# Value parts of an exact linear-attention stage: GpSimd's work given to VectorE, ScalarE and TensorE, pair by pair of key tiles

## The reference

```python
q, k, v = heads(x @ Wq + bq), heads(x @ Wk + bk), heads(x @ Wv + bv)
q_proj, k_proj = proj(q), proj(k)      # gelu(x @ W1 + b1) @ W2 + b2, to 16 columns: one number per token and head
# both centred by their mean over tokens and divided by a common std
Z = concatenate([k_proj, q_proj])      # one key per token and head
vc = v - mean(v over tokens)
context(i) = sum over k_j < q_i of vc_j * (q_i - k_j)      # written as a sort and cumulative sums
norm(i)    = 2 * sum over k_j < q_i of (q_i - k_j) - (q_i * count - sum of k)
out = 2 * context / max(norm, 1e-4)
```

## Time and profile before

| | |
|---|---|
| median of three runs | 1470.56 us (1470.32 to 1474.03) |
| profiled execution, its own time | 1472.39 us |
| its span, first to last instruction | 1470.8 us |
| TensorE, VectorE, ScalarE, GpSimd busy | 74%, 65%, 55%, 45% |
| granted TensorE clock, mean | 0.882 of full |

### The profile page before, as it was taken

How to read it: one execution, slowest core, us unless ns; L and a number is a source line. 1 busy time by engine, 2 the same in 40 slices (tenths; PEclk the granted TensorE clock), 3 DMA queues, 4 the chain that set the end, 5 groups by cost and what they waited for, 6 DMA issues and landing times. The chain is left out here.

```text
span 1470.8 us, 30026 instructions
## 1 busy us (share of the span) xinstructions
PE 1088.7 (74%) x12088; PEld 893.4 (61%) x12088; DVE 957.1 (65%) x1553; ACT 811.8 (55%) x909; POOL 664.6 (45%) x648
## 2 busy tenths in 40 slices
PE   5364789368989899909998986465547965976698
PEld 2153665368888897609888883254227962642597
DVE  4212645799999975489999996223833644764365
ACT  6211443389999933249999995322523325653233
POOL 3744000736666640174666662745072440327244
PEclk9688799779999999959999997777778996987799
DMA  9777200402122100101212112265333433003343
GB/s 259 281 212 249 76 1 0 184 30 88 59 88 83 65 1 0 53 9 59 88 59 88 63 56 87 105 203 171 105 130 88 123 105 116 1 1 112 95 127 102
DMA packets 84587, 140.59 MB, mean 96 GB/s; under 512 B 10574, under 2 KB 71246, under 8 KB 79950
## 3 DMA queue, kind: packets, MB, share of 16 engines
q1 hardware_dynamic: 70276, 102.15, 21.8%
q0 software_dynamic: 13056, 35.87, 6.7%
q10 hardware_dynamic: 1120, 0.66, 0.2%
HBM read 86.62 MB, written 56.27 MB: 97 GB/s over the span
## 5 line engine op out<-in xcount | busy, mean ns | idle before, releaser
L1186 ACT ACTIVATE b_signs<-b_q_everywhere,normed 128x2048 bf16<-128x2048 f32 x224 | 429.8, 1991 | 23.6 <-PE banks L1096 20.7
L1096 PE MATMUL banks<-b_value_parts,b_signs 128*128 128x102 bf16 x8192 | 392.1, 209 | 38.7 <-DVE b_signs L1332 36.1
L1096 PEld LDWEIGHTS banks<-b_value_parts,b_signs 128*128 128x128 bf16 x8192 | 376.0, 97 | 61.8 <-DVE b_signs L1332 56.1
L1332 DVE TENSOR_SCALAR b_signs<-b_q_everywhere,normed 128x2048 bf16<-128x2048 f32 x288 | 395.9, 1435 | 1.6 <-PE banks L1096 1.6
L558 POOL DMA_INDIRECT moe_slots<-normed,slot_of_token x128 | 124.7, 974 | 39.3 <-issue 33.2
L1390 POOL TENSOR_TENSOR normed<-b_sums,normed 128x16 f32<-128x16 f32 x32 | 35.0, 1095 | 135.0 <-DVE b_sums L1343 135.0
L371 PE MATMUL banks<-identity,normed 128*128 128x128 f32 x256 | 51.5, 337 | 57.6 <-ACT normed L347 57.6
L1366 POOL TENSOR_TENSOR b_signs<-b_signs,normed 128x1024 f32<-128x1024 f32 x8 | 22.0, 2755 | 157.6 <-DVE normed L1282 157.1
L320 DVE BATCH_NORM_STATS2 ln_stats<-residual 128x6 f32<-128x256 f32 x192 | 71.1, 417 | 21.5 <-SPq L1589 10.5
L1088 PE MATMUL banks<-normed,ones_bf 128*128 128x408 bf16 x128 | 28.9, 350 | 69.5 <-DVE normed L1300 69.5
L380 PE MATMUL banks<-normed_T,wg 128*8 128x256 f32 x256 | 77.8, 433 | 0.0
(11 more groups left out here) (254 smaller groups left out, 2424.2 us busy)
## 6 DMA issues: line engine op xcount, KB each, us to landing
b_q_everywhere<-q_rows SPq DMA_DIRECT2D x32, 1024.0 KB, 4.7
normed<-expert_rows SPq DMA_DIRECT2D x6, 1024.0 KB, 10.4
d_rows<-moe_slots SPq DMA_DIRECT2D x40, 129.5 KB, 2.2
f_rows<-moe_slots SPq DMA_DIRECT2D x40, 129.5 KB, 2.2
moe_slots<-a_empty SPq DMA_DIRECT2D x8, 518.0 KB, 10.1
a_rows<-moe_slots SPq DMA_DIRECT2D x16, 259.0 KB, 3.6
moe_empty_slots<-a_empty SPq DMA_DIRECT2D x8, 518.0 KB, 5.5
moe_slots<-moe_empty_slots SPq DMA_DIRECT2D x1, 4144.0 KB
```

Of the source, the lines that this page charges most:

```text
L1096: ins = nc.tensor.matmul(banks[qt // QPB][:, qt % QPB * VP:(qt % QPB + 1) * VP], t.SG[:, (hh * TB + kt) % RING, qt * P:(qt + 1) * P], t.VO ...
L1186: nc.scalar.activation(t.SG[:, g % RING, :], t.QB[:, hh % 2, :], ACT.Sign, bias=t.NKT[:, kt, hh % H:hh % H + 1]).then_inc(s.sign_a, 1)
L1332: nc.vector.tensor_scalar(t.SG[:, g % RING, :], t.QB[:, hh % 2, :], t.KTM[:, kt, hh % H:hh % H + 1], 2.0, ALU.is_gt, ALU.mult).then_inc(s. ...
```

## The change

The row work of GpSimd in the preparation goes. The values of a pair of key tiles are held in a PSUM bank (seven banks in turn), with the centring row already added there by a bf16 product of a matrix with ones in its first three rows (`ROWS3B`) and the row's three parts in three partitions (`ROWP`, made by `dve_row`). Per pair, ScalarE copies the high part out of the bank; VectorE writes the product with k (`VZ`) and the rest of the values (`VR`, four slots); ScalarE writes both middle parts and the product's high part; TensorE makes rest minus middle part in the same bank by an f32 product with the identity and a bf16 one with its negative (`MINUSI`), and ScalarE copies that out as the third part; VectorE writes the product's third part. The column of k itself is split once for all tiles, and GpSimd only sets the columns of ones. The totals are 64 products with ones or minus ones over the finished parts (`pe_held`), ahead of head 0's first product, into banks 4 to 7; VectorE reduces and splits them behind its sign of tile 6 (`dve_held`). The products that add the totals stand ahead of tile 15 in each head and no longer ahead of tile 0. Scores of k are normed and transposed first, those of q later; SyncE's first broadcast waits for these. At the start GpSimd makes three constants more.

```diff
@@ program start, GpSimd
+    nc.gpsimd.memset(k.MINUSB[:, :], -1.0)
...
+    nc.gpsimd.tensor_copy(k.ROWS3B[:, :], k.LAYERF[:, 0, :])
+    nc.gpsimd.tensor_scalar(k.MINUSI[:, :], k.IDENT[:, :], -1.0, None, ALU.mult)
@@ pe_prepare, TensorE
-    pe_values(k, batch, 0)
-    pe_values(k, batch, 1)
+    pe_parts(k, batch)
+def pe_parts(k, batch):
+    nc.tensor.wait_ge(s.row, batch + 1)
+    for p in range(4):
+        pe_value(k, batch, p)
+    nc.tensor.wait_ge(s.zk, batch + 1)
+    for tile in range(TB):
+        ins = nc.tensor.transpose(k.bank[4][:, tile * H:(tile + 1) * H], t.Z[:, 1, tile * P:(tile + 1) * P], k.IDENT[0:H, 0:H])
+    ins.then_inc(s.zkt, 1)
+    pe_value(k, batch, 4)
+    for n in range(PAIRS + 1):
+        if n == 1:
...
+            for tile in range(TB):
...
+        if n + 5 < PAIRS:
+            if n + 5 >= 7:
+                nc.tensor.wait_ge(s.a_third, at + n - 1)
+            pe_value(k, batch, n + 5)
+        if n >= 1:
+            nc.tensor.wait_ge(s.a_mid, at + n)
+            nc.tensor.matmul(value_bank(k, n - 1)[:, :], k.IDENT[:, :], t.VR[:, (n - 1) % 4, :], start=True, stop=False)
+            nc.tensor.matmul(value_bank(k, n - 1)[:, :], k.MINUSI[:, :], value_columns(t, n - 1, False, 1), start=False,
+                             stop=True).then_inc(s.a_left, 1)
+def pe_held(k, batch):
...
+    for tiles, lo, hi, ones in ((ACT_KT, 0, 2 * DH, k.ONESB), (DVE_KT, 2 * DH, VC, k.MINUSB)):
+        for tile in tiles:
+            for b in range(4):
...
@@ pe_head
-        nc.tensor.wait_ge(s.held_parts, batch + 1)
...
+        pe_held(k, batch)
...
     for kt in range(TB):
+        if kt == TB - 1:
+            if h == 0:
+                nc.tensor.wait_ge(s.held_parts, batch + 1)
+            for bank in banks:
...
@@ act_prepare, ScalarE
+    for p in range(4):
+        act_part(k, batch, p, 0)
+    for n in range(PAIRS + 1):
...
+        if n < PAIRS:
+            act_product(k, batch, n, 0)
+            if n + 4 < PAIRS:
+                act_part(k, batch, n + 4, 0)
+            act_part(k, batch, n, 1)
+        if n >= 1:
+            act_product(k, batch, n - 1, 1)
+            act_part(k, batch, n - 1, 2)
@@ dve_prepare, VectorE
+    for n in range(PAIRS + 2):
+        if n < PAIRS:
+            nc.vector.wait_ge(s.a_hi, at + n + 1)
...
+            if n >= 4:
+                nc.vector.wait_ge(s.a_left, at + n - 3)
...
+        if 1 <= n <= PAIRS:
+            nc.vector.wait_ge(s.b_hi, at + n)
...
+        if n >= 2:
+            nc.vector.wait_ge(s.b_mid, at + n - 1)
...
+def dve_held(k, batch):
+    nc.vector.wait_ge(s.held_mm, batch + 1)
+    nc.vector.tensor_reduce(t.HELD[:, :, :].rearrange("p (b i) c -> p b i c", i=4),
+                            k.half[1][:, :, 0:4 * VP].rearrange("p b (i n c) -> p b i c n", i=4, n=3), AX_X, ALU.add).then_inc(s.held, 1)
...
+def dve_row(k):
...
@@ pool_attention, GpSimd
-        for g in range(TB // 4):
...
+        nc.gpsimd.wait_ge(s.rows_t, 16 * (batch + 1))
+        nc.gpsimd.memset(t.VOP[:, :, :, 2 * DH], 1.0)
+        nc.gpsimd.memset(t.VOP[:, :, :, VC + 2 * DH], 0.0)
+        nc.gpsimd.memset(t.VOP[:, :, :, 2 * VC + 2 * DH], 0.0).then_inc(s.ones_set, 1)
```

More of the change, by code:

```diff
@@ L112 @@
     "att_in bqk_in at_xn at_turned at_xt w1_hi w1_lo mb proj hm mean row rows_t rows_hi rows hid gt score z zvar zstd "
-    "zq zk zq_stored vmm val ztr nkt u_made held hi rest mid third held_parts "
+    "zq zk zq_stored vmm vz zkt zqt qtm nkt ones_set kz_hi kz_rest kz_mid kz_third "
+    "a_hi a_rest a_mid a_left a_third b_hi b_rest b_mid b_third held_mm held held_parts "
     "qb_in0 qb_in1 sign_d sign_a acc sum nf n2 ctx "
@@ new lines, in pe_value @@
+def pe_value(k, batch, p):
+    nc, s, t = k.nc, k.s, k.at
+    for i in range(2):
+        tile = 2 * p + i
+        for c in range(KD):
+            nc.tensor.matmul(value_bank(k, p)[:, i * D:(i + 1) * D], t.XT[batch][:, c, tile * P:(tile + 1) * P], t.W["wv"][:, c, :],
+                             start=(i == 0 and c == 0), stop=False)
+    nc.tensor.matmul(value_bank(k, p)[:, :].rearrange("p (i d) -> p i d", i=2), k.ROWS3B[:, :],
+                     t.ROWP.unsqueeze(1).broadcast_to([P, 2, D]), start=False, stop=True).then_inc(s.vmm, 1)
@@ L1207, in dve_attention @@
                 dve_sign(k, hh, kt)
+                if h == 0 and kt == 6:
+                    dve_held(k, batch)
                 if h and kt == 2:
@@ L1261, in dve_prepare @@
             nc.vector.wait_ge(s.mean, batch + 1)
-            step(nc.vector.tensor_tensor(t.ROW[:, 1, :], k.bank[5][:, 0:D], t.BVB[:, :], ALU.add))
-            nc.vector.tensor_tensor(t.ROW[:, 0, :], t.BVB[:, :], t.ROW[:, 1, :], ALU.subtract).then_inc(s.row, 1)
+            dve_row(k)
     k.vs.until(mark)
@@ L1283, in dve_prepare @@
                             ALU.mult).then_inc(s.nkt, 1)
-    for g in range(TB // 4):
-        u, rows = value_rows(t, g)
-        nc.vector.wait_ge(s.held, 4 * batch + g + 1)
-        for n in range(2):
-            nc.vector.wait_ge(s.hi, 8 * batch + 2 * g + n + 1)
-            nc.vector.tensor_tensor(u[n], u[n], rows(n, 0), ALU.subtract).then_inc(s.rest, 1)
-        for n in range(2):
-            nc.vector.wait_ge(s.mid, 8 * batch + 2 * g + n + 1)
-            nc.vector.tensor_tensor(rows(n, 2), u[n], rows(n, 1), ALU.subtract).then_inc(s.third, 1)
-        if g + 2 < TB // 4:
-            nc.vector.wait_ge(s.third, 8 * batch + 2 * g + 2)
-            dve_values(k, batch, g + 2)
@@ new lines, in dve_held @@
+def dve_held(k, batch):
+    nc, s, t, step = k.nc, k.s, k.at, k.vs.step
+    part = lambda i: t.HELD3[:, :, i * VC:(i + 1) * VC]
+    nc.vector.wait_ge(s.held_mm, batch + 1)
+    nc.vector.tensor_reduce(t.HELD[:, :, :].rearrange("p (b i) c -> p b i c", i=4),
+                            k.half[1][:, :, 0:4 * VP].rearrange("p b (i n c) -> p b i c n", i=4, n=3), AX_X, ALU.add).then_inc(s.held, 1)
+    nc.vector.wait_ge(s.held, batch + 1)
+    step(nc.vector.tensor_scalar(part(0), t.HELD[:, :, :], 1.0 / P, None, ALU.mult))
+    step(nc.vector.scalar_tensor_tensor(out=t.HELD[:, :, :], in0=t.HELD[:, :, :], scalar=1.0 / P, in1=part(0),
+                                        op0=ALU.mult, op1=ALU.subtract))
```

181 lines of the change are left out of this document (100 added, 81 removed).

## The result

The changed kernel takes 1455.12 us (median of four runs, 1451.94 to 1457.44); the kernel before, on the same chip, 1470.66 us (four runs, 1470.32 to 1474.03). The ratio is 0.9888, 95% interval 0.9862 to 0.9914: faster by 1.1%, 15.5 us where 11.4 were forecast. 1455.12 lies between the forecast (1459.2) and the rival "better than forecast" (1452.8). The profiled execution took 1457.44, span 1456.1.

What follows compares the result with a forecast made beforehand. VectorE's list bounds the unchanged head loop, so gains come from preparation: parts 11.7 us sooner, 5.5 given back, 6.2 a batch. 2 x 6.2 - 2 x 0.2 - 0.6 = 11.4 us less, 1459.2; eight in ten, 1452 to 1469.

Steps and rivals of the forecast that it cites:

- better than forecast: Rival: parts end at 291, totals take 5.5 us, gain 9.4 us a batch, whole time 1452.8; chance 0.12.
- Steps 1 and 5: Centring vector: 0.35 us reaches the last two scores; head 0: sum starts 14.8 us after the totals.
- Step 5: Head 0: sum 14.8 us after the totals; products moved to tile 15 cost 0.2 us at each batch's end.
- Step 3: Parts of the values in eight pairs: 21.8 us of VectorE work plus waits, ending 11.7 us sooner.
- Step 4: Totals as 64 products on TensorE before head 0: 7.3 us, all on the path; bounds 5.5 and 12.8.
- Step 6: Kernel start: three more GpSimd operations before `a_empty` is filled delay the first scatter by 0.6 us.
- The totals that eat the gain: Rival: totals take 12.8 us with parts ending at 295, 4.7 us slower in all, 1475; chance 0.09.
- The hand-over bound: Rival: crossings between engines pace the pairs, parts end at about 298, whole time near 1470; chance 0.09.

Runs made afterwards that it cites:

- experiment 3: Changed kernel with the four products that add the totals back ahead of the first tile in every head but head 0; 1478.41 us.
- Experiment 1: Changed kernel with VectorE writing the values' third part, without TensorE's residue products and ScalarE's third copies; 1486.49 us beside 1497.44 for the kernel before.
- experiment 8: Changed kernel with ScalarE's copy of the third part one round later; 1472.94 us, ratio 0.9823 to the kernel before.
- experiment 7: Changed kernel with totals' products inside the rounds of the parts, k column's split on GpSimd and new constants made late; 1473.21 us, ratio 0.9836 to kernel before.
- experiment 9: Changed kernel with totals inside the rounds, k column and late constants on GpSimd, and third copy one round later; 1480.82 us, ratio 0.9825 to kernel before.
- experiment 4: Kernel before, keeping its values and parts, but with totals made by TensorE and GpSimd's row additions removed; 1498.42 us beside 1497.44.
- experiment 2: Changed kernel with the 64 products of the totals made twice; interval from centring vector to head 0's sum 68.23 and 68.24 us.
- experiment 6: Changed kernel with the totals' products of finished pairs issued inside the rounds of the parts; 1469.81 us, ratio 0.9806 to the kernel before.

## Why the prediction was right, and where it was off

**Steps 1 and 5 held to a few hundredths.** The second score begins 2.72 us later than in the earlier trace rows (252.78 to 255.50), of which 2.37 were there at the centring vector: 0.35, as forecast. From the last part to the totals 0.19 us (0.2 forecast), from the first head tile to the sum 14.73 (14.8). That the loop doesn't change from head to head was forecast and is shown by the period and by experiment 3; at the last head the moved products cost 0.5 us a batch, where Step 5 had 0.2.

**Step 3 came out right in its sum.** VectorE's first product starts 16.29 us behind the centring vector (16.84 forecast, 266.2 less 249.36), and from there it takes 26.11 us (26.2 forecast). Its list is 22.2 us instead of 21.8, and it waits 3.9 instead of 3.4 plus 1.0. So the parts end 12.3 us sooner, where the forecast had 11.7. Two prices in the list were off and cancelled, which was luck: an operation of 512 columns took 0.60 us from start to start, not 0.645, and the column of k cost more (its last step 1.33 us). Of the first product's 0.55 some 0.2 was the prediction's own rounding up: four pairs at 2.03 from 255.85 end at 263.97, not 264.2. What the prediction put less well is the reason: behind the first rounds it said that all "goes at VectorE's pace". Experiment 1 shows that VectorE's list can grow by its 3.9 us of waits for nothing, experiment 8 shortens the parts by 1.6 us through ScalarE's side alone, and experiment 7 by 2 us through work taken off ScalarE and VectorE both. The pace is set by three lists that are nearly equal and wait for each other; the sum came out because the waits had been put in.

**Step 4 is the term that was mis-sized.** 7.3 us were taken and 5.45 measured, the low bound of 5.5. The price at full clock was the low end of its 5.5 to 6.9: 28 products of 384 columns in 4.54 us (294.32 to 298.86) and 36 of 24 columns in 0.91. The 1.9 us on top were for half a chance of half the clock, and the clock stayed at 1.00. How the two make 7.3 isn't written out: the middle of its 5.5 to 6.9 with half of the 1.9 gives 7.15, the low end with the whole of it 7.4. So the clock is the larger part of the miss, between 0.95 and 1.9 us, and the price at full clock, at its low end, is the rest. This step explains 1.85 of the 2.57 us a batch by which the interval is better than forecast (65.34 by the prediction's own steps); 0.55 is the earlier first product, the rest rounding. Experiment 1 shows that the doubt was about a real thing: take the residues out, and the totals cost 7.5 to 8.0. Two batches of 2.57 are 5.1 us, and the result was 4.1 better than the forecast.
The outputs in short runs cost nothing that shows: 0.162 us for 384 columns is 2.37 columns a nanosecond, hardly under the 2.4 GHz that this clock level is. The rule against non-contiguous PSUM access, which Step 4 cites, isn't borne out by this for runs of 32 columns; for runs of 2 no row here has a price to compare the 0.025 us a product with. The Trainium skill has the rule a second time (Advanced Engine Details and Errata, section "PSUM Cachelines"), and there adds that every two consecutive elements should be contiguous for the best rate; by that addition, the trace agrees, as both outputs have such runs.

**Step 6 isn't borne out.** `a_empty` is filled 0.93 us later (0.6 forecast), at 5.81 instead of 4.88. But that this comes through isn't shown. The first scatter's row stands at 33.58 instead of 32.16, and in the seven other profiles with the late fill between 32.01 and 35.88; with the constants made late and the fill back at 4.89 and 4.88 (experiments 7 and 9), it stands at 32.77 and 34.61. The centring vector came no sooner in these two than in the changed kernel on the same chip (259.19 for 257.38, and 260.82 for 258.45). So the 2.37 us can't be laid to the constants; between profiles of the same code this stretch differs by more.

**Between the batches 2.08 us were lost.** 0.5 of them are the moved products at the last head (experiment 3). The other 1.6 no step foresaw: a stretch of half clock, 558.9 to 562.4, in batch 1's preparation (the row of 560.00 above, six products in 2 us). In the kernel before, the clock is 1.00 all the way between its first sum and its second vector; the same work stands 6 us later there, and has eleven products in 2 us:
```profile
566.00:568.00 2.00, 2.00 (x11) 1.63 (x10) 0.96 (x2) 1.97 (x3) 0.00 (x0) 1.00 0.00 0
```
From the first sum to the second vector it took 285.2 to 285.3 us in all three profiles of the changed kernel, and 284.7 and 285.2 in experiments 3 and 4, where the half clock came too; it took 283.7 in the six other experiments, where it didn't. The code of that preparation is the same in all of them. What brings it on is open: it isn't the length of the interval alone, since experiments 2 and 4 have the same interval (68.2, 68.3), one without and one with it.

**The rivals.** "Better than forecast" named the right cause, totals at 5.5 us, and came within 0.6 us of the gain a batch (9.4 for 8.85); it counted nothing for the losses outside. The totals that eat the gain are what experiment 4 nearly shows, with the old values kept. The hand-over bound did not come, since the first sign is at 42.40 and not at 48.

**What would be faster still.** Experiments 6 to 9 have ratios of 0.9806, 0.9836, 0.9823 and 0.9825 with intervals that overlap each other and those of the changed kernel (0.9867 and 0.9866), so a gain in the whole time isn't settled for any of them. Inside the stage it is clear, 1.4 to 5.2 us a batch; each median is 6 to 9 us below that of the changed kernel on its chip. Every run of experiment 6 was faster than every run of the changed kernel beside it, if barely at the edge (1474.47 at most, 1474.5 at least). By its intervals experiment 9 should beat experiment 6 by 7 us (2 x 3.5); in the whole this doesn't show, as the stretches outside scatter between profiles on one chip: the end by 3 to 4 us, the start by 2 to 9.

## What to carry to other kernels

When work moves onto an engine that then has the path to itself, count what that engine does just before as part of the price: here small products ahead of it kept TensorE's clock full and saved over 2 us of the work behind them, at the price of some waits for them (1.91 and 1.34 us on ScalarE). Where three engines pass each pair of tiles around with nearly equal lists, sum the longest list and its waits together; shortening one list or one wait gave a part of its size here, and two such edits did not add up. Read a change of 1% by an interval that begins and ends inside the changed stage, since the stretches around it scattered by 2 to 9 us between profiles of one chip and the change was worth 15. Take care that it ends where the change's last effect does: this one ended at the first sum and missed 0.5 us at the sixteenth.

## What the runs showed of the hardware that was not expected

Single bf16 elements 204 bytes apart are dear. ScalarE's copy of 256 of them took 1.39 us at 270.50 and 1.36 at 282.72 (Step 3's sum of 20.5 leaves 0.35 for each), VectorE's write of 256 took 1.33 us (the row of 287.38 above), where the same operation with its strided operand read instead of written took 0.65 and one on contiguous rows 0.43. On GpSimd the same cast took 1.36 us and 1.81:
```profile
275.62 1.36 POOL L1495 CAST b_value_parts<-normed 128x256 bf16<-128x256 f32 x1 [18.58 <-DVE normed L1386]
277.06 0.86 POOL L1496 TENSOR_TENSOR normed<-normed,b_value_parts 128x256 f32<-128x256 f32 x1
277.98 1.81 POOL L1497 CAST b_value_parts<-normed 128x256 bf16<-128x256 f32 x1
```
The Trainium skill (Advanced Engine Details and Errata, section "SBUF Cachelines") says that accesses which each fall into another 16-byte line are penalised; by that rule, the trace agrees, and it adds the size. Moved to GpSimd, which stood idle, this column gave about 2 us a batch, by the estimate in experiment 7. The granted clock of TensorE can fall or stay at the same gap: 1.85 us idle brought it down in both batches of experiment 6. With the changed kernel's own code up to there, 1.84 us left it full in nine batches (six of the changed kernel, two of experiment 2, batch 1 of experiment 3) and brought it down in a tenth, batch 0 of experiment 3, where it stood at half from 287.3 to 290.8.
